# A linear-attention kernel on one core: load of x and store of y move from SyncE's queue to ScalarE's, with a new order of work on every engine

## The reference

```python
x = x + 0.5 * ffn(layernorm(x))            # x1; of the ffn its final normalisation with gain ln_g and shift ln_b
q, k, v = (layernorm(x) @ W.T for W in (Wq, Wk, Wv))      # 16 heads of 32
phi_q, phi_k = elu(q) + 1, elu(k) + 1
S = cumsum(phi_k[:, None] * v[None, :]); z = cumsum(phi_k)          # along the 4096 positions
x = x + (phi_q @ S / (phi_q . z + 1e-5)) @ Wo.T + bo
x = x + 0.5 * ffn(layernorm(x))
```

## Time and profile before

| | |
|---|---|
| runs of the kernel before | 1024.25, 1025.33, 1025.99 us; median 1025.33 us |
| profiled execution | 1025.5 us, of which 1023.8 us are the span from the first to the last instruction |
| mean granted clock of TensorE | 0.962 of full speed |
| busy share of the span | PE 89%, DVE 82%, ACT 74%, POOL 70% |

### The profile page before, as it was taken

How to read it: one execution, slowest core, us unless ns; L and a number is a source line. 1 busy time by engine, 2 the same in 40 slices (tenths; PEclk the granted TensorE clock), 3 DMA queues, 4 the chain that set the end, 5 groups by cost and what they waited for, 6 DMA issues and landing times.

```text
span 1023.8 us, 29832 instructions
## 1 busy us (share of the span) xinstructions
PE 909.5 (89%) x10240; PEld 524.7 (51%) x10240; DVE 837.4 (82%) x1513; ACT 757.8 (74%) x1327; POOL 714.4 (70%) x879
## 2 busy tenths in 40 slices
PE   1468999999999999999999999999999999999974
PEld 1234555555555555555555555555455555555542
DVE  3466988888888888988888889888888888878763
ACT  4367877788777777887777778877777788778761
POOL 1136877867787778777777787777677777767762
PEclk8678999999999999999999999999999999999996
DMA  7145678876666677666666777566577756667872
GB/s 256 21 71 100 133 135 163 166 143 120 141 143 139 138 164 164 145 126 133 139 140 137 163 164 144 123 137 139 126 150 164 161 131 119 137 131 126 142 125 62
DMA packets 421405, 139.81 MB, mean 137 GB/s; under 512 B 402544, under 2 KB 402544, under 8 KB 421360
## 3 DMA queue, kind: packets, MB, share of 16 engines
q1 hardware_dynamic: 421360, 139.24, 66.1%
HBM read 21.76 MB, written 16.78 MB: 38 GB/s over the span
## 4 chain that ended last, share of the span: by engine, by line
PE 57%; DMA 15%; SPq 8%; issue 6%; DVE 6%; ACT 4%; POOL 0%; ACTq 0%; DVEq 0%; POOLq 0%
PE PJ L1125 40%; DMA XT<-XH 14%; PE AV L1198 7%; SPq L333 3%; PE SC L1175 3%; PE AV L1210 3%; PE AV L1195 2%; DVE ATTN L968 2%; PE PJ L1224 2%; DVE TP L949 2%; ACT ATTN L679 1%; SPq L286 1%; SPq L341 1%; SPq L322 1%; ACT DEN L671 1%
## 5 line engine op out<-in xcount | busy, mean ns | idle before, releaser
L1125 PE MATMUL PJ<-wT,XT 128*128 128x512 f16 x2304 | 535.6, 385 | 61.2 <-DMA XT<-XH 51.6
L1125 PEld LDWEIGHTS PJ<-wT,XT 128*128 128x128 f16 x2304 | 217.1, 99 | 320.4 <-DMA XT<-XH 63.1
L472 POOL TENSOR_TENSOR A<-AM,A 128x512 f16<-128x512 f32 x256 | 291.1, 1157 | 12.2 <-ACT A L652 12.2
L652 ACT ACTIVATE A<-AM 128x512 f16<-128x512 f32 x256 | 151.3, 634 | 43.1 <-DVE AM L891 41.6
L1224 PE MATMUL PJ<-wT,AT 128*128 128x512 f16 x768 | 179.0, 383 | 1.6 <-DMA AT<-ATTN 1.6
L464 POOL TENSOR_SCALAR_AFFINE_SELECT AM<-AM 128x512 f32<-128x512 f32 x128 | 81.4, 636 | 105.0 <-ACT AM L642 102.6
L1224 PEld LDWEIGHTS PJ<-wT,AT 128*128 128x128 f16 x768 | 72.9, 99 | 80.2 <-issue 3.5
L1198 PE MATMUL AV<-VN,A 128*128 128x33 f16 x3072 | 112.8, 178 | 0.0
L1195 PE MATMUL AV<-SS,QS 128*128 128x33 f16 x1024 | 109.7, 178 | 3.2 <-POOL A L472 3.2
L1198 PEld LDWEIGHTS AV<-VN,A 128*128 128x128 f16 x3072 | 107.7, 96 | 3.7
L602 ACT ACTIVATE PHI<-PJ,inv_scale 128x512 f32<-128x512 f32 x64 | 43.6, 681 | 79.4 <-PE PJ L1125 79.4
(11 more groups left out here) (98 smaller groups left out, 1529.7 us busy)
## 6 DMA issues: line engine op xcount, KB each, us to landing
X<-in_L_attn_x_dram SPq DMA_DIRECT2D x32, 512.0 KB, 4.2
out_dram<-Y SPq DMA_DIRECT2D x32, 512.0 KB, 4.9
A<-in_L_attn_Wk_dram SPq DMA_DIRECT2D x1, 1024.0 KB, 7.8
A<-in_L_attn_Wq_dram SPq DMA_DIRECT2D x1, 1024.0 KB, 10.1
QS<-in_L_attn_Wv_dram SPq DMA_DIRECT2D x1, 1024.0 KB, 12.2
QS<-in_L_attn_Wo_dram SPq DMA_DIRECT2D x1, 1024.0 KB, 14.4
XT<-XH SPq DMA_TRANSPOSE x64, 4.4
KS<-KN SPq DMA_TRANSPOSE x64, 4.3
```

The lines of the kernel that those rows point to most:

```text
L472: g.tensor_tensor(A[:, b, LO, hg], AM[:, k % 4], A[:, b, HI, hg], ALU.subtract).then_inc(a_lo.sem, 1)
L652: a.activation(A[:, b, HI, hg], AM[:, k % 4], ACT.Copy).then_inc(a_hi.sem, 1)
L1125: ins = t_.matmul(PJ[b], XT[:, w, c, b * C:(b + 1) * C], wT[m_][:, m, c, :], start=(c, w, m) == todo[0], stop=(c, w, m) == todo[-1])
```

## The change

The load of the next chunk of x and the store of y are issued by ACT, in ACT's own queue; SP issues turns only. Apart from that, the operations and their waits are the same, and the lists of all engines are put in another order. In the cyclic order of PE, `scores(1, 3)` comes after `attend(0, 0)`, and `update(1, *)` after `scores(0, 3)`; in POOL's, `x1_bias` comes after `split_a(0, 2)`, `split_s(0)` and `spread_k(1)` move. In the diff, "..." stands for lines left out; each list is a `body(st)`, whose first two lines are left out, and indentation is cut.

```diff
--- before.py
+++ after.py
@@ -249,7 +249,7 @@
         def pair_wait(eng, sems, st, ahead, by):
 eng.wait_ge(sems[st.parity(ahead)], st.pair(ahead, by))
 
-        passed = {e: sem(f"passed_{e}") for e in ("sp", "pool", "dve")}
+        passed = {e: sem(f"passed_{e}") for e in ("sp", "pool", "dve", "act")}
 
         def stand(eng, name):
 
@@ -277,14 +277,6 @@
     PROJECT, ATTEND, FRONT, FINISH = st.has(1), st.has(0), st.has(2), st.has(-1)
 
     class Ops:
-        def next_x():
...
         def turn_x(b):
             if not FRONT:
                 return
@@ -333,30 +325,20 @@
             sp.dma_start_transpose(AT[:, b].rearrange("p f (c t) -> p (f c) t", t=C),
                                    ATTN[:, b].rearrange("p f e -> p (f e)")).then_inc(attn_turned[b].sem, 16)
 
-        def store_y():
...
     return Ops
 
 def body(st):
-    prev.turn_k(0)
     prev.turn_q(0)
     prev.turn_attn(0)
     prev.turn_q(1)
     prev.turn_attn(1)
-    prev.next_x()
-    prev.store_y()
     prev.turn_x(0)
     prev.turn_x(1)
     prev.turn_k(1)
+    now.turn_k(0)
 
 first = ops(Step(0, -2))
-first.next_x()
 first.turn_x(0)
 first.turn_x(1)
 run(sp, body)
@@ -498,27 +480,27 @@
 
 def body(st):
-    prev.spread_k(0)
     prev.cut(1, 3)
-    prev.split_a(1, 0)
     prev.spread_q(0)
     prev.split_a(1, 1)
     prev.split_a(1, 2)
     prev.split_a(1, 3)
     prev.spread_q(1)
-    prev.split_s(0)
     prev.rstd1_of_x1()
+    now.cut(0, 1)
+    prev.spread_k(1)
     now.rstd0_of_x()
-    prev.spread_k(1)
-    now.cut(0, 1)
     now.split_a(0, 0)
     now.split_a(0, 1)
+    now.split_a(0, 2)
+    now.x1_bias()
     now.cut(0, 3)
-    now.x1_bias()
     now.rstd2_of_x2()
-    now.split_a(0, 2)
+    prev.split_s(0)
     now.split_a(0, 3)
     now.cut(1, 1)
+    now.split_a(1, 0)
+    now.spread_k(0)
     prev.split_s(1)
 
 first = ops(Step(0, -2))
@@ -555,6 +537,21 @@
     PROJECT, ATTEND, FRONT, FINISH = st.has(1), st.has(0), st.has(2), st.has(-1)
 
     class Ops:
+        def next_x():
+            if not st.has(4) or (st.number and st.chunk(4) < 2):
+                return
+            wait(act, x_gained, f, 1)
+            stand(act, "act")
+            start = st.chunk(4) * C
+            a.dma_start(X[:, st.parity(4)], x[:, bass.ds(start, C), :].rearrange("b p e -> p b e")).then_inc(x_loaded[st.parity(4)], 16)
+
+        def store_y():
+            if not FINISH:
+                return
+            wait(act, y_done, back, 1)
+            stand(act, "act")
+            a.dma_start(out[:, bass.ds(back * C, C), :].rearrange("b p e -> p b e"), Y[:]).then_inc(y_stored.sem, 16)
+
         def front_scale(b):
             if not FRONT:
                 return
@@ -691,46 +688,48 @@
 def body(st):
-    prev.split_a(1, 0)
+    prev.copy_scores(1, 3)
+    prev.back_scale(1)
     prev.sums(0)
     prev.q_half(0)
     prev.split_a(1, 1)
     prev.split_a(1, 2)
-    prev.split_a(1, 3)
     prev.exp_relu_q(1)
     if following:
         w_half(3)
+    prev.split_a(1, 3)
     prev.attn_half(0)
-    prev.s_half(0)
     prev.q_half(1)
-    prev.k_half(1)
     prev.sums(1)
     prev.v_half(0)
+    prev.normalise(0)
     prev.attn_half(1)
-    prev.normalise(0)
+    prev.k_half(1)
+    prev.x_half(0)
+    prev.v_half(1)
+    now.copy_scores(0, 1)
     prev.normalise(1)
-    prev.v_half(1)
-    prev.x_half(0)
     prev.x_half(1)
-    now.copy_scores(0, 1)
+    now.copy_scores(0, 3)
+    now.split_a(0, 0)
+    prev.store_y()
     now.front_scale(0)
-    now.split_a(0, 0)
     now.split_a(0, 1)
-    now.copy_scores(0, 3)
     now.split_a(0, 2)
     now.front_scale(1)
+    prev.s_half(0)
     prev.s_half(1)
+    now.exp_relu_k(0)
     now.split_a(0, 3)
-    now.exp_relu_k(0)
+    now.next_x()
+    now.k_half(0)
     now.back_scale(0)
-    now.back_scale(1)
-    now.k_half(0)
+    now.copy_scores(1, 1)
     now.exp_relu_k(1)
     if opening:
         w_half(2)
-    now.copy_scores(1, 1)
+    now.split_a(1, 0)
     now.exp_relu_q(0)
-    now.copy_scores(1, 3)
 
 square(0)
 square(1)
@@ -739,6 +738,7 @@
 first.front_scale(0)
 first.front_scale(1)
 square(2)
+first.next_x()
 first.normalise(0)
 first.normalise(1)
 w_half(0)
@@ -1020,22 +1020,20 @@
 def body(st):
-    prev.phi_q(0)
+    prev.back_y(0)
+    prev.reciprocals(0)
+    prev.quotient(0)
+    prev.front_mean1(0)
+    prev.low_q(0)
     now.front_stats(0)
-    prev.reciprocals(0)
-    prev.mask(1, 2)
-    prev.front_mean1(0)
-    prev.quotient(0)
-    prev.low_q(0)
-    prev.front_stats1(1)
-    now.front_mean(0)
-    prev.add_s(0)
+    prev.front_mean1(1)
+    now.front_stats(1)
     prev.phi_q(1)
     if following:
         w_low(3)
-    prev.front_mean1(1)
+    prev.add_s(0)
     prev.attn_low(0)
-    now.front_stats(1)
+    prev.back_gain(1)
     prev.low_q(1)
     prev.back_y(1)
     prev.reciprocals(1)
@@ -1043,33 +1041,35 @@
     prev.low_v(0)
     prev.attn_low(1)
     prev.low_k(1)
+    now.mask(0, 0)
+    prev.x_low(0)
+    now.front_mean(0)
     now.front_mean(1)
-    now.mask(0, 0)
+    prev.low_v(1)
+    now.mask(0, 2)
+    prev.x_low(1)
     prev.add_s(1)
-    prev.x_low(0)
-    prev.low_v(1)
     prev.add_out(0)
-    prev.x_low(1)
+    now.front_gain(0)
+    prev.add_out(1)
+    now.front_gain(1)
     prev.out_stats(0)
-    now.mask(0, 2)
-    prev.add_out(1)
-    now.front_gain(0)
+    prev.out_stats(1)
     prev.out_mean(0)
-    now.front_gain(1)
-    prev.out_stats(1)
     prev.out_mean(1)
     now.front_x1(0)
+    now.phi_k(0)
     now.front_x1(1)
-    now.phi_k(0)
+    now.front_stats1(0)
+    now.front_stats1(1)
+    now.mask(1, 0)
     now.back_gain(0)
-    now.back_gain(1)
-    now.mask(1, 0)
     now.low_k(0)
-    now.back_y(0)
-    now.front_stats1(0)
+    now.mask(1, 2)
     now.phi_k(1)
     if opening:
         w_low(2)
+    now.phi_q(0)
 
 first = ops(Step(0, -2))
 first.front_stats(0)
@@ -1230,6 +1230,8 @@
 def body(st):
+    prev.scores(1, 3)
+    prev.attend(0, 1)
     prev.project_q(1)
     if following:
         w_transposes(3 * GROUPS, 4 * GROUPS)
@@ -1240,12 +1242,12 @@
     prev.attend(1, 1)
     prev.project_v(1)
     now.scores(0, 0)
-    prev.update(1, 0)
-    prev.update(1, 1)
     now.scores(0, 1)
     prev.project_out(0)
     now.scores(0, 2)
     now.scores(0, 3)
+    prev.update(1, 0)
+    prev.update(1, 1)
     prev.project_out(1)
     now.project_k(0)
     now.project_k(1)
@@ -1255,9 +1257,7 @@
     now.scores(1, 1)
     now.project_q(0)
     now.scores(1, 2)
-    now.scores(1, 3)
     now.attend(0, 0)
-    now.attend(0, 1)
 
 w_transposes(0, 2 * GROUPS)
 run(pe, body)
```

## The result

The changed kernel takes **969.24 us** (median of 4 runs, 968.30 to 970.58). The kernel before took 1025.66 us on the same chip. The ratio is 0.9451, with an interval of 0.9433 to 0.9469, so the change is worth 5.5%. The forecast was 978 us.

A forecast was written before the change was run, and what follows sets the result against it. PE's work, 27.4 us a step, was the floor, with waits for XT making it 29.39. Sum: 1023.8 - 53.7 - 1.7 + 9.5 - 1.5 = 976.4 us span, forecast 978 us; range 966 to 1002.

The forecast's parts named there:

- Part (1): Load and store leave SP's queue: XT(0) has 1.2 us to spare, its wait goes (-53.7 us), slow start goes (-1.7).
- the scatter: Allowance for uneven steps with little to spare in the new orders: 0.35 us a step, +9.5 us.
- Part (2): Load and store issued on ACT, store overlapping XT(1) and KS(1): 0 to 0.9 us a step, taken as 0.
- Only SP's issue time is won: Rival: XT's turn still takes 5.2 us, only 0.3 us a step before its issue goes; 1017 us, chance 0.03.
- Part (3): ACT issues two DMAs a step; an issue costs ACT 0 to 0.65 us, at worst 1.4, taken as 0.3.
- d: Cost of a DMA issue on ACT: 0 to 0.65 us, at worst 1.4, taken as 0.3.
- the gap on ACT is d: Sign to check: the gap on ACT before front_scale(0) and before k_half(0) is d.
- Part (4): New orders make two long chains from scores(0, 3); at d = 0.3 neither is late by over 0.1 us.
- Chain A: From scores(0, 3) over ACT, POOL, DVE to project_q(1): 13.4 + d against PE's 13.6 us, late by d - 0.2.
- Chain B: From scores(0, 3) to project_v(1): 20.6 + 2d against PE's 21.2 us, late by 2d - 0.65.
- the five places: phi_k(1), low_q(1), the last split before attend(1, 1), XT(1) and KS(1): less than 0.7 us to spare at each.
- Part (5): Both ends: mask(1, 0) before back_gain shortens PE's 4.3 us wait after the loop; -1.5 us, bounds +1 and -4.

The follow-up runs named there:

- run 9: Kernel before, all issues in place, but load and store carry 8 of the 128 rows (32 KB each instead of 512 KB): 969.91 us, ratio 0.9469.
- run 3: Kernel before, with load and store moved within SP's queue to behind the turns of XH and KN: 977.11 us, ratio 0.9498.
- run 1: Kernel before in its old orders; ACT issues the store after split_a(0, 0) and the load after split_a(0, 3): 1000.29 us, ratio 0.9716.
- run 4: Kernel before in its old orders; ACT issues load and store right after x_half(1), about when SP did: 1017.13 us, ratio 0.9876.
- run 5: Kernel before in its old orders; ACT issues both store and load after split_a(0, 3): 1021.75 us, ratio 0.9990.
- run 6: Changed kernel, with the store moved earlier in ACT's order, from behind split_a(0, 0) to behind v_half(1): 994.91 us, ratio 0.9716.
- run 8: Changed kernel's orders; SP issues load and store in its one queue, behind XH's turns and KN's for b = 1: 968.34 us, ratio 0.9451.
- run 7: Changed kernel, with load and store each issued as two 256 KB transfers, so ACT issues four DMAs a step: 981.18 us, ratio 0.9582.
- run 11: Changed kernel, with POOL's x1_bias moved ahead of split_a(0, 2): 982.07 us, ratio 0.9589.
- run 2: Changed kernel's new orders, with load and store back in SP's queue ahead of XT(0): 1034.38 us, ratio 1.0047.

## Why the prediction was right, and where it was not

The measured 969.24 us lies in the forecast's own band of 968 to 985, near its low end.

- **The cause of XT's wait.** Right: the transfer, not SP's issue. Runs 9 and 3 show it from two sides. Its sum was read a little wrong: of XT's 51.6 us only 46.0 lie in the 27 steps that were to hold 53.7 us of waits; the rest of the 53.7 is as above, slow matmuls and some 0.2 us a step that no row notes as a wait.
- **Part (1), XT(0) in time.** It gave 4.8 us from the end of `x_low(0)` to `project_k(0)`; 4.7 were measured. XT(0) landed at 520.81, 3.0 us after its issue and 1.5 ahead of `project_k(0)`. The turn is no longer waited for, and `project_k(0)` takes its 5.34 us: -53.7 and -1.7 stand, before the scatter. That the slow start at 904.98 came "after the longest wait of these steps" is not so: the waits at 141.41 and 200.98 were 2.32 and 2.38 us, and the matmuls behind them took 5.35.
- **Part (2), contention at 0.** The number is right (0.04 us a step), the reason that it gave is not. It said that nothing is lost by the order of transfers, since the queue carries the sum of them at their own rates. Runs 1, 4, 5 and 6 show that this sum hides who is late: PE waits 0.9 us for XT(0) with the store beside it, 1.4 with the load too, 1.8 for KS(1) beside both, 0.6 for AT(1) beside the store. It costs nothing in the changed kernel only because both transfers fall where the turns beside them have time: XT(1), beside the store, takes 3.7 us (4.6 forecast) in place of 3.1, and KS(1) lands 1.0 us ahead of `scores(1, 0)`. So the 0 rested on the places of the change, not on the reason given, and that is in part luck. Its bound for KS(1), 4.9 us to landing, was passed in run 5 (6.8). The prediction's places, 2.2 us ahead of `project_k(0)` and 5 us behind it, were 2.8 and 4.6, both a little earlier and without harm.
- **"Only SP's issue time is won".** The prediction gave this rival 1017 us, and said that the rule of the Trainium skill ("DMA: Bandwidth & Descriptors", Issuing engines are not separate DMA queues) leads to it. The changed kernel refutes the time, not the rule: run 4, which moves the issuer and not the moment, is at 1017.13 us, and the turn stays at 5.4 us. The trace agrees with the rule that all issuers share the engines: XT(0) takes 4.9 us beside a store from ACT's queue (run 1), where it takes 3.0 alone. What the changed kernel gains comes from another moment for the transfer, and a place further back in the one queue gives that too (run 8).
- **Part (3), d = 0.3.** Mis-sized: it is 0 for one issue behind a running activation (spacing 0.52 us), and 0.43 for a second one in a row (run 7). Its test "the gap on ACT is d" was right for `front_scale(0)`; for `k_half(0)` a gap of 0.22 us is put down to DVE's PHI, so it says nothing of d.
- **Part (4), chains A and B.** Their price at d = 0 is nothing, as their sums say (A -0.2, B -0.65). Run 7 is the test of the sums: with a second issue at both places A and B both give a step of 27.6 for a d of 0.43 (late by 0.23 and 0.21), and it grows to 27.9. Chain A is borne out: `project_q(1)` is 0.24 us later. The other 0.2 us are the wait for POOL's last splits before `attend(1, 0)` and `attend(1, 1)`, one of the five places that the prediction named as tight but gave no sum; it is the wait of run 11 too. Chain B is not tested, as PE stood still ahead of its end for longer than B is late.
- **The scatter, +9.5.** The term that was mis-sized most; all that stood for its size was one pair of starts, 28.9 us apart against a mean of 29.4. The steps take 27.54 us in place of the sum's 27.4 + 0.35, so the scatter is 3.9 us in all, and 5.6 of the 9.5 did not come. Of the 3.9, the first five steps hold 2.3 (139.30 us, to the start at 247.94) and the last one 0.7; the 21 between take 27.44 each.
- **Part (5), ends -1.5.** They gave 2.85 ahead of the first `project_k(0)` and 1.25 in the tail behind the last two steps: -4.1. The wait for AM fell from 4.8 to 1.1 us as it said, but of those 3.7 us only a third came out: the longest wait for POOL's A in the tail grew from 2.1 to 3.3 us, that for KS from 1.0 to 2.2. Of the 2.85 us at the start, 1.7 are one projection of the third step: its 12 matmuls took 4.44 us at 71.91 in the kernel before (granted clock 0.61 from there to 76.30), and take 2.75 at 71.58 in the changed one (1.00). That was no part of the forecast, so the start came out by luck; the rest of it I did not follow.

The sum again: 5.6 (scatter) + 2.6 (ends) + 0.1 are the 8.3 us between the 976.4 us span of the sum and the 968.1 measured.

What the 5.5% are made of: the same two lines moved in SP's queue give 5.0% (run 3), and moved in the new orders 5.5% (run 8); the two intervals overlap, so the half per cent between them rests on the steps of the profiles, 27.70 and 27.48 us. What the new orders are worth depends on where load and store go: 0.3% without their bytes, 0.5% behind the turns, nothing with the megabyte ahead of XT(0) (run 2), and 2.7% with the two places on ACT (0.9716 to 0.9451), which are the change's. With the old orders the megabyte still costs 27.70 - 27.49 = 0.21 us a step behind KS(1), with the new ones 0.04. No run beat the changed kernel by more than the noise; what is left of a step, 27.44 us in the middle, is PE's own work.

## What to carry to other kernels

When a transfer on the path is slow, ask what is in flight beside it, in any queue, before asking who issues it; taking the bytes away while all issues stay in place is a cheap test that separates bandwidth from issue time. A bulk transfer that nobody waits for still has a right place in the step: after the urgent turn, and far enough ahead of the next one; list each turn with its slack before moving it, not only the one that waits now (run 5 lost the whole gain to the next turn). Moving two lines within a queue may be worth nearly as much as a second queue and new orders on every engine. A wait can cost more than its idle time, when the clock is low behind it: look at the duration of the first matmuls after it.

## What the runs showed of the hardware

- A turn of 3.0 to 3.5 us takes 4.9 us beside a store of 512 KB from another queue, and 5.4 us beside load and store; KS(1) took 6.8 beside both in place of 4.4. From one queue or from two, the price is about the same (5.22 and 5.4 us).
- A DMA issue on ACT of 0.4 us did not delay ACT's next operation where an activation of 0.6 us was running (spacing 0.52 us); a second issue in a row added 0.43 us (run 7).
- After some waits of PE the granted clock stood at its lower level (0.5, 1.2 GHz) for a stretch: behind 1.97 and 2.14 us of waiting 24 matmuls took 7.04 us (727.16 and 904.98, kernel before), behind 3.81 us 7.96 (run 2), in place of 5.35. Other waits of the same length, 2.32 and 2.38 us (141.41 and 200.98, kernel before), were followed by full speed.
- The issue of a load takes SP 0.39 us for 512 KB and 0.29 us for 32 KB: the size made 0.10 us of it.
- Issued behind three turns in one queue (run 3), the load took SP 0.82 us to issue, and load and store landed after 4.9 and 5.1 us (medians), with nobody waiting for them; from ACT's queue in the changed kernel they took 3.5 and 3.1.
